# Causal ban of four score groups per batch: added by VectorE inside the maxima instead of by TensorE

## What is computed

```
def _L0_attn_ref(x, w_qkv, w_out):          # x: 16 batches of 256 tokens, 16 heads of 16
    qkv = (x @ w_qkv).reshape(b, s, 3, HEADS, HEAD_DIM)
    q, k, v = qkv[:, :, 0] / sqrt(HEAD_DIM), qkv[:, :, 1], qkv[:, :, 2]
    scores = einsum('bqhd,bkhd->bhqk', q, k)
    scores = where(causal_mask, scores, NEG)
    attn = softmax(scores, axis=-1)
    return einsum('bhqk,bkhd->bqhd', attn, v).reshape(b, s, HIDDEN) @ w_out
```

## Time and profile before

| | |
|---|---|
| median of 3 runs | 808.99 us |
| the profiled execution: its time | 809.38 us |
| its span, first to last instruction | 807.6 us |
| around the span (809.38 - 807.6) | 1.8 us |
| mean granted TensorE clock, share of full speed | 0.894 |
| busy: TensorE matmul / VectorE / ScalarE / GpSimd | 645.4 / 556.8 / 380.2 / 402.0 us |
| attention with its scores, 238 to 558 us | 320 us |

### The profile page before, as it was taken

How to read it: one execution, slowest core, us unless ns; L and a number is a source line. 1 busy time by engine, 2 the same in 40 slices (tenths; PEclk the granted TensorE clock), 3 DMA queues, 4 the chain that set the end, 5 groups by cost and what they waited for, 6 DMA issues and landing times.

```text
span 807.6 us, 18608 instructions
## 1 busy us (share of the span) xinstructions
PE 645.4 (80%) x5484; PEld 524.9 (65%) x5501; DVE 556.8 (69%) x1560; ACT 380.2 (47%) x962; POOL 402.0 (50%) x466
## 2 busy tenths in 40 slices
PE   2623999998768999999999999987823999999300
PEld 2412899997646777777777777764612999988200
DVE  7888455554657888888888887753787455567543
ACT  2520466664324555555555555545800566655100
POOL 5101566666453554555555532224017777666674
PEclk9855899999979999999999999999955899999755
DMA  8770455556663444444444433310603566775754
GB/s 261 266 256 19 132 169 170 170 171 147 140 176 106 121 122 118 118 124 122 124 123 125 122 111 86 108 29 2 210 19 88 164 194 188 157 182 164 235 156 123
DMA packets 94158, 113.46 MB, mean 140 GB/s; under 512 B 11648, under 2 KB 84624, under 8 KB 94096
## 3 DMA queue, kind: packets, MB, share of 16 engines
q1 hardware_dynamic: 80240, 74.87, 29.2%
q0 software_dynamic: 13824, 37.77, 19.3%
q10 hardware_dynamic: 32, 0.02, 0.0%
HBM read 49.30 MB, written 33.55 MB: 103 GB/s over the span
## 4 chain that ended last, share of the span: by engine, by line
PE 69%; DVE 14%; POOL 6%; issue 4%; DMA 3%; ACT 2%; DVEq 1%; another core or an unknown queue 0%; POOLq 0%; SPq 0%; ACTq 0%
PE bank L863 17%; PE bank L870 8%; PE bank L413 6%; PE bank L472 6%; PE bank L458 5%; PE bank L433 5%; PE bank L420 4%; PE bank L853 4%; POOL shared L704 4%; PE bank L492 3%; PE bank L436 3%; PE bank L480 1%; PE bank L792 1%; DVE shared L1201 1%; POOL gathered_rows L339 1%
## 5 line engine op out<-in xcount | busy, mean ns | idle before, releaser
L863 PE MATMUL bank<-xeT,shared 128*128 128x128 f32 x1280 | 174.0, 280 | 2.3 <-ACT xeT L970 1.2
L693 POOL DMA_INDIRECT shared<-normed,source x112 | 110.7, 988 | 104.0 <-DVE source L1231 50.4
L863 PEld LDWEIGHTS bank<-xeT,shared 128*128 128x128 f32 x1280 | 160.0, 196 | 3.6 <-issue 1.8
L363 POOL TENSOR_SCALAR_AFFINE_SELECT pr<-pr 128x512 f32<-128x512 f32 x128 | 80.9, 655 | 157.1 <-ACT pr L530 157.0
L583 DVE TENSOR_REDUCE mx<-bank 128x2 f32<-128x512 f32 (+1 forms) x192 | 128.0, 686 | 26.6 <-PE bank L436 21.0
L530 ACT ACTIVATE pr<-bank 128x512 f32<-128x512 f32 x192 | 102.8, 609 | 31.9 <-PE bank L458 19.7
L1250 DVE TENSOR_TENSOR hid<-bank,silu 128x128 f32<-128x128 f32 x160 | 46.5, 290 | 101.8 <-ACT silu L974 100.8
L870 PE MATMUL bank<-wd_sb,hid 128*128 x320 | 98.0, 389 | 0.7 <-DVE hid L1250 0.5
L984 ACT COPY shared<-wgu_sb 128x256 f32 x160 | 63.5, 397 | 66.0 <-DVE source L1231 65.9
L974 ACT ACTIVATE silu<-bank 128x128 f32<-128x128 f32 x160 | 44.3, 277 | 77.6 <-PE bank L863 77.0
L704 POOL DMA_INDIRECT shared<-grouped_out,slot x64 | 62.9, 983 | 32.1 <-issue 16.7
(11 more groups left out here) (175 smaller groups left out, 1116.8 us busy)
## 6 DMA issues: line engine op xcount, KB each, us to landing
grouped_out<-shared SPq DMA_DIRECT2D x160, 128.0 KB
shared<-parts SPq DMA_DIRECT2D x154, 128.0 KB, 2.3
spare<-parts SPq DMA_DIRECT2D x70, 128.0 KB, 2.3
normed<-shared SPq DMA_DIRECT2D x16, 512.0 KB, 3.6
wgu_sb<-_L_ffn_gate_up_proj_dram SPq DMA_DIRECT2D x8, 512.0 KB, 8.8
out_dram<-x_sb SPq DMA_DIRECT2D x16, 256.0 KB, 3.0
x_sb<-in_L_attn_x_dram SPq DMA_DIRECT2D x3, 1024.0 KB, 10.1
wd_sb<-in_L_ffn_down_proj_dram SPq DMA_DIRECT2D x4, 512.0 KB, 9.2
```

The source lines that it names most:

```text
L363: nc.gpsimd.affine_select(out=m, in_=m, compare_op=ALU.is_ge, fill=0.0, base=0, pattern=[[0, 4], [1, P]], channel_multiplier=-1).then_inc( ...
L693: nc.gpsimd.indirect_dma_start(xe[f][r], None, normed, bass.IndirectOffsetOnAxis(source[:, j:j + 1], 0)).then_inc(arrival(f, r), 16)
L863: last = nc.tensor.matmul(bank[2 + u][:, h * P:(h + 1) * P], wgu_tile[f][:, u, c, h * I:(h + 1) * I], xeT[:, u, c, :], start=(c == 0), sto ...
```

## The change

For groups 4 to 7 of each batch, the line 436 matmul (and its weight load) is left out, and the last of the two line 433 matmuls increments `score_done`. On VectorE, the one reduction over 512 columns of these groups becomes two `tensor_tensor_reduce` instructions, one for each head. Each reads 256 columns of scores from PSUM and 256 of a new fp32 constant `later_keys` in SBUF, adds them, writes the sum back over the scores, and gives the maximum of the row to one column of `mx`. GpSimd makes `later_keys` at the start with one more memset and one more select, and the waits for the constants count to 5. The orders on the engines, and groups 0 to 3 and 8 to 11, stay as they are.

```diff
+        later_keys = sb("later_keys", [P, 2, P])
...
-            pe.wait_ge(att_consts, 4)
+            pe.wait_ge(att_consts, 5)
...
                     for i in range(nh):
-                        nc.tensor.matmul(dst[:, i * w:(i + 1) * w], q[0:ROWS, h0 + i, u * P:(u + 1) * P], k[0:ROWS, h0 + i, 0:w],
-                                         start=(i == 0), stop=False, skip_group_check=True)
+                        last = nc.tensor.matmul(dst[:, i * w:(i + 1) * w], q[0:ROWS, h0 + i, u * P:(u + 1) * P], k[0:ROWS, h0 + i, 0:w],
+                                                start=(i == 0), stop=4 <= n < 8 and i == nh - 1, skip_group_check=True)
+                    if 4 <= n < 8:
+                        last.then_inc(at["score_done"], 1)
+                        return
                     diag = dst[:, :].rearrange("p (h k) -> p h k", k=w)[:, :, u * P:(u + 1) * P]
...
         def attn_vector(dve):
 
+            dve.wait_ge(att_consts, 5)
...
                 after(dve, at["score_done"], 3 * G * b + n + 1)
+                if 4 <= n < 8:
+                    for i in range(nh):
+                        scores = bank[3 + n % 2][:, i * S:(i + 1) * S]
+                        last = nc.vector.tensor_tensor_reduce(scores, scores, later_keys[:, :, :].rearrange("p k n -> p (k n)"), 1.0, NEG,
+                                                              ALU.add, ALU.max, mx[:, u, h0 + i:h0 + i + 1])
+                    last.then_inc(at["max_ready"], 1)
+                    return
                 nc.vector.tensor_reduce(mx[:, u, h0:h0 + nh], bank[3 + n % 2][:, :].rearrange("p (h k) -> p h k", h=nh),
                                         AX.X, ALU.max).then_inc(at["max_ready"], 1)
...
+            nc.gpsimd.memset(later_keys[:, :, :], 0.0).then_inc(const_step, 1)
...
+            nc.gpsimd.affine_select(out=later_keys[:, 1, :], in_=later_keys[:, 1, :], compare_op=ALU.is_ge, fill=NEG,
+                                    base=0, pattern=[[-1, P]], channel_multiplier=1).then_inc(att_consts, 1)
```

More of the change, by code:

```diff
@@ L762, in _ @@
             nc.gpsimd.memset(future[:, :, :], 0.0).then_inc(const_step, 1)
+            nc.gpsimd.memset(later_keys[:, :, :], 0.0).then_inc(const_step, 1)
             for i in range(2):
                 nc.gpsimd.memset(v_sb[i][:, :, :, :], 0.0).then_inc(const_step, 1)
-            pool.wait_ge(const_step, 7)
+            pool.wait_ge(const_step, 8)
             nc.gpsimd.affine_select(out=ident_b[:, :], in_=ident_b[:, :], compare_op=ALU.not_equal, fill=1.0,
```

## The result

Eleven runs of the changed kernel gave a median of 810.63 us, eleven of the kernel before 808.86 us: the ratio is 1.0025, with a 95% interval from 1.0014 to 1.0037. So it is slower by 1.8 us (0.2%), and not by the 13 us that were forecast. The profiled execution has a span of 809.0 us.

What follows compares the result with a forecast made beforehand. TensorE was taken to bound the attention periods. 14 batches at +0.83 us (11.6) plus 1.4 us in the first gave +13.0 on 809.38, forecast as 822 us, 1.6% slower; the range ran from 806 to 838 us.

Steps and rivals of the forecast that it cites:

- The bound, and the place: TensorE bounds the 19.84 us period; VectorE's 2.96 us idle lies mostly late, only 0.18 us between groups 4 and 9.
- There is no slack at all here: Group 7 on TensorE: group 5's maxima are done at 440.54 and the load starts at 440.55.
- g: The time a group takes from VectorE with the change; 0.60 us before, forecast at 0.94.
- 4g - 2.49: TensorE's standing time per batch, in us, waiting for VectorE's maxima ahead of groups 7 and 9.
- What is removed: Four line 436 matmuls per batch on TensorE, 0.11 us each: 0.44 us per batch.
- What it adds: VectorE's new instructions in groups 4 to 7: g bounded from 0.68 to 1.40 us, 0.94 taken between 0.86 and 1.02.
- lower bound of 0.68: Cheap-instruction rival on VectorE: the maximum comes out with the main part, g = 0.68 us, 806.4 us in all; chance 0.13.
- 4g - 2.93: Net change per batch, TensorE's stall less its 0.44 us saving: +0.83 us at g = 0.94, nothing at 0.73.
- What follows in the period: VectorE's MIX, groups 8 and 9, LOW_K and MOMENTS start 1.36 us later; idle time ahead of the projections absorbs the remaining 0.21.
- a g near 0.73, within 0.2%: Case where VectorE's time per group leaves the whole time within 0.2% of no change; chance 0.08.
- No overlap: Rival: VectorE operations delivering a maximum don't overlap, g = 1.18 us, 836.4 us in all; chance 0.12.
- half rate: Rival: the value carried along the row costs VectorE two cycles per column, g = 1.40 us, 849.6 us; chance 0.10.

Runs made afterwards that it cites:

- e9: e2 with GpSimd's causal selects cut to 4 of 128 columns of each head: 852.2 us, ratio 0.9886 to the kernel before; usual period 19.47 us.
- e8: The changed kernel with one more VectorE maximum over 128 columns in each of groups 4 to 7: 873.25 us against 859.11 for the kernel before.
- e10: The changed kernel with GpSimd's selects cut to 4 of 128 columns of each head: 859.75 us, ratio 0.9987; usual period 19.97 us.
- e2: The kernel before without the diagonal matmuls of groups 4 to 7, keeping VectorE's plain maxima: 808.74 us, ratio 0.9986.
- e4: The changed kernel with LEFT_K and LOW_Q moved behind group 7 in VectorE's order: 817.94 us, ratio 1.0105, periods of 20.58 us.
- e11: e4 with GpSimd's selects cut to 4 of 128 columns of each head: 856.22 us, ratio 0.9950; usual period 19.83 us.
- e12: The kernel before without the diagonal matmul in all 12 groups, with plain maxima: 851.37 us against 860.93, ratio 0.9899.
- e5: e2 with MIX moved behind group 9 and LOW_K in VectorE's order: 864.22 us, ratio 1.0059 to the kernel before.

## Why the prediction was wrong, by its own steps

- **The bound, and the place.** Right. TensorE bounded the periods, VectorE's idle time lay outside the stretch from group 4 to group 9, and after the change TensorE waits ahead of groups 7 and 9 and hardly anywhere else. "There is no slack at all here" for group 7 is what the 0.32 us show. At the measured g the sum 4g - 2.49 gives a wait of 0.49 us, and 0.51 were measured.
- **What is removed.** Right: 0.11 us for each matmul. e9, where nothing else is in the way, wins 0.37 of the 0.44 us per period.
- **What it adds: the step that failed.** "I take the middle, g = 0.94." The term was mis-sized; g measured 0.745. Both of the values that I took the middle of charged the read of the accumulator with 0.09 us at least. It takes about 0.04: main instructions stand 0.38 us apart, against 0.34 for a plain operation. By the prediction's own sign ("if g lies outside 0.79 to 1.08") the forecast is wrong. The rule of the Trainium skill that I cited ("VectorE: DVE Perf Modes", section "Two Vector instructions with no wait between them") agrees with the trace, which has two instructions for each head; but a count of instructions isn't a price. The "middle" was the middle of two guesses above the truth, when the lower bound of 0.68 was nearer.
- **Why so little carries so far.** The net is 4g - 2.93 us per period, so 0.2 us in g is 0.8 us in the period and 11 us in the time. For g = 0.745 it gives +0.05 us per period, and 0.13 were measured. Of the missing 0.08, 0.06 is a second, small slip: the replay has a result ready 0.08 us behind the next start, as a reduction is, but the accumulator read ends 0.14 behind it. With the first batch's 4 x 0.145 = 0.6 the sum would have been about +1.3 us, with +1.8 measured. e8 tests the same formula at the other end.
- **What follows in the period.** I moved MIX by the queue's delay and kept its length. In the trace of before GpSimd's selects start 0.36 us before MIX ends, so the two overlapped already. In the changed kernel they start 0.08 us behind the start of MIX's second half (445.37 against 445.29) in place of 0.52 us, and this half takes 0.37 us longer. This missed step cost nothing there (e10). In e2 and e4 it decided the period (e9, e11), in e12 it may have.
- **Rivals.** The real value fell beside the case with 8 chances in 100, "a g near 0.73, within 0.2%". No overlap and half rate didn't happen.
- **The range.** It began at 806 and held 810.63; the direction was right and the size, 13.0 us against 1.8, was not. That it came out above zero at all hangs on hundredths of g, and there is luck in it.

## What to carry to other kernels

Where engines hand work over in a fixed order, replay the two queues side by side and write the result as a formula in the unknown duration before choosing a value: here it crosses zero at 0.73 us, amid the plausible values, and that alone should have moved chances from "slower" to "no change". The same exchange of TensorE's work for VectorE's is a gain or a loss by its place in the queue: ask where the receiving engine has idle time, and how soon the other engine needs the result. VectorE had 0.32 us ahead of group 10; in groups 4 to 7 it had 0.18, and group 7's load started as soon as the maxima that it needs were done. And where two engines overlap on something that they share, look at who waits today: after a small change it can be the other.

## What the runs showed of the hardware that was not expected

- An accumulator read is 0.14 us long in the profile and takes about 0.04 us of VectorE's time (0.38 against 0.34 between starts).
- VectorE operations with two operands in SBUF stretch when GpSimd's select runs: MIX's second half, a pair of operations, took 0.88 us with no select beside it (e5), 1.25 where it met the first of two selects in the changed kernel, and 2.03 in e2, where it ended 0.29 us after both selects were over. In the kernel before it was GpSimd that lost (1.44 us for two selects in place of 1.22), although the selects started as far behind the start of this half as in e2 (0.52 and 0.51 us); what decides it isn't shown. With the selects cut short (e9) it is 0.475 us per operation again. That agrees with the Trainium skill, "SBUF — State Buffer", section "Who interferes with whom", which says that a VectorE instruction with two SBUF inputs contends with a GpSimd instruction that reads SBUF. The new instructions, with one operand in PSUM, kept their length: in the changed kernel they take 0.42 to 0.47 us with a select beside them and without.
- Attention periods agree to 0.01 us on chips whose whole times differ by 50 us (19.47 us in e9 and in the fast periods of e2, 19.97 in the changed kernel and e10).
